# Graph network kernel: where the marks of the lanes are made, and ten instead of eight of GpSimd's 25 partial sums

## The chip, the cores and the metric

The kernel runs on one core of a Trainium2 chip. The time is that of the whole program in microseconds, the median of several executions. In profiles the engines are called PE (TensorE, matrix products), DVE (VectorE), ACT (ScalarE), POOL (GpSimd) and SP (SyncE, which only issues transfers here). PEld is the loading of TensorE's weights.

## What is computed

A graph of 3125 nodes with 128 features and 100,000 edges, sorted by their destination, goes through a mean layer, three attention layers, an aggregation layer with four statistics (PNA) and two more mean layers. The change touches the first mean layer and the bookkeeping that the later passes need from it:

```python
h = relu(layernorm(x))
agg = segment_sum(h[src], dst)               # mean over a node's incoming edges
deg = segment_sum(ones, dst)                 # how many edges a node has
mean = agg / max(deg, 1)
x = x + relu(where(deg > 0, mean, h) @ W.T + b)
# then three times:
h = attention(h, src, dst)                   # softmax over a node's incoming edges
```

## The kernel before, in words

**First mean pass.** The edges have first been turned into a matrix of counts, A (source by destination), which lies in DRAM. The pass reads A in seven blocks, 0 to 6: six of 512 destination nodes (four tiles of 128 nodes, 6400 KB) and one of 128. Two buffers in SBUF take turns; a buffer is loaded again when TensorE, VectorE and GpSimd have all read it. Inside a block, the 25 source tiles lie side by side. Per block:

- TensorE multiplies features by counts over the 25 source tiles (`neighbour_sums`, line 1043), then sums the column sums over the partitions with a matrix of ones into `psL` (line 1139: every partition then holds the in-degrees of the block's nodes as a row) and, transposed, into `psS` (line 1142: degrees as columns), then makes the previous block's outputs tile by tile (`node_outputs`, lines 1056 and 1057). Two PSUM banks take turns for the tiles, so the third tile of a block waits until VectorE has used up the first.
- VectorE sums 17 of the 25 source tiles per destination (`degrees`, line 1540), GpSimd the other 8 (lines 647 and 650, seven adds), and VectorE puts the two together (line 1545). Then VectorE works on the block before: `segments`, then `outputs` (lines 1579 to 1581, three instructions a tile), then `moments` (lines 1332 and 1335) for the next layer norm.
- ScalarE copies TensorE's sums out of PSUM (`sums_out`, line 753).

**The marks.** Every one of the 128 partitions ("lanes") later works on 784 consecutive edges. `pick` says for each lane and node whether the node's last edge lies in the next lane, that is, whether the node's edges cross the lane's end. `segments` makes it from a running sum of the degree row: a scan (line 1554), a carry (1556), a difference (1557), three comparisons (1561 to 1563). The scan and the difference read the row in `psL`. Between them and after them stand the small operations on the degrees as columns (`deg`, `has`, `nohas`, `hrec`). After the pass TensorE turns `pick` into one number a node, the crossing flag (line 1152, 25 products, `psH`), and VectorE makes `cbias` of it (line 1629). `pick` is first used by the pass after that at the end of the first attention pass.

**Attention pass.** Each of the three attention passes has 56 groups of 14 steps of all lanes, four groups a round, in four slots of SBUF; two groups are a pair. GpSimd fetches the source rows of a group by indirect transfers (line 695), 12 of the 14 steps in even slots, 11 in odd ones. TensorE fetches the rest of a pair from SBUF by one-hot products (`fetch`, line 1187), whose one-hot matrices ScalarE (`own_hots`, lines 871 and 876) and VectorE (line 1694) make. VectorE reduces the fetched rows (line 1718), makes the logits (lines 1743 to 1760), ScalarE takes their exponentials (line 900), and VectorE runs the recurrence over the steps (lines 1768 to 1778). The order on each engine is the order of the code. The indices of a slot reach GpSimd through ScalarE (`window`, lines 851 to 854): those of slots 0 and 1 ahead of the pass, those of slot 2 in ScalarE's group 0, ahead of its exponential, and those of slot 3 in its group 1, so behind the exponential of group 0.

Of the kernel before, what the change touches and what calls it, by code (L numbers as in the profile page):

```python
# [29 lines left out]
POOL_S = 8  # L30
# [63 lines left out]
def build(nc, x, src, dst, W0, b0, Ws, Wd, att_s, att_d, gat_b, M_w, M_b, U_w, U_b, gamma, beta,  # L94
# [37 lines left out]
    with ExitStack() as ctx:  # L132
# [97 lines left out]
        psF = [psT[0], psT[1], psY[0], psY[1], psL, psZ, psS]  # L230
        cw_p = psH[:, 0:15 * H].rearrange("p (h k) -> p h k", h=H)
# [163 lines left out]
        dense_ps, mb_rdy, red_rdy, deg_ps = sem("dense_ps"), sem("mb_rdy"), sem("red_rdy"), sem("deg_ps")  # L395
        deg_used, node_out_ps, node_out = sem("deg_used"), sem("node_out_ps"), sem("node_out")
# [318 lines left out]
        def _(act):  # L715
# [83 lines left out]
            for b in range(NBK):  # L799
                sums_out(0, b)  # L800
            act.wait_ge(deg_rdy, 1)
# [218 lines left out]
        def _(pe):  # L1020
# [111 lines left out]
            for b in range(NBK + 1):  # L1132
                if b < NBK:
                    neighbour_sums(0, b, u)
                    n = blocks[b][1] * W
                    pe.wait_ge(red_rdy, b + 1)
                    if b:
                        pe.wait_ge(deg_used, b)
                    nc.tensor.matmul(psL[:, 0:n], ones[:], reds[b % 2][:, 0:n], start=True, stop=True)
                    for t in tiles(b):  # L1140
                        k = t - TPB * b
                        ins = nc.tensor.matmul(psS[:, 32 + t:33 + t], reds[b % 2][:, k * P:(k + 1) * P], ones[:, 0:1],
                                               start=True, stop=True)
                    ins.then_inc(deg_ps, 1)
                if b:
                    node_outputs(0, b - 1)
# [3 lines left out]
            pe.wait_ge(pick_rdy, NBK)  # L1150
            for t in range(NT):
                ins = nc.tensor.matmul(psH[:, t:t + 1], pick_t(t), ones[:, 0:1], start=True, stop=True)
            ins.then_inc(cross_ps, 1)
            pe.wait_ge(node_out, NT)

            for p in passes:
# [55 lines left out]
                if p.by_pe:  # L1212
                    pe.wait_ge(split_rdy, p.splits0 + 5)
                    for q in range(p.groups // 2):
                        fetch(q)

# [93 lines left out]
        def _(dve):  # L1310
# [236 lines left out]
            def segments(b):  # L1547

                a, n = blocks[b][0] * W, blocks[b][1] * W
                at = slice(tiles(b)[0], tiles(b)[-1] + 1)  # L1550
                dve.wait_ge(deg_ps, b + 1)
                if b:
                    dve.wait_ge(node_out, tiles(b - 1)[-1] + 1)
                link(v.tensor_tensor_scan(upto[:, 0:n], ones[:, 0:1].broadcast_to([P, n]), psL[:, 0:n], carry[:, 0:1],
                                          ALU.mult, ALU.add))
                link(v.tensor_copy(carry[:], upto[:, n - 1:n]))
                link(v.tensor_tensor(since[:, 0:n], upto[:, 0:n], psL[:, 0:n], ALU.subtract))
                link(v.tensor_copy(deg[:, at], psS[:, 32 + at.start:32 + at.stop]))
                v.tensor_scalar(tmp[:, 0, at], deg[:, at], 1.0, None, ALU.max).then_inc(deg_used, 1)
                pk = pick[:, a:a + n]  # L1560
# [3 lines left out]
                dve.wait_ge(deg_used, b + 1)  # L1564
                v.tensor_scalar(has[:, at], deg[:, at], 0.0, None, ALU.is_gt)
                link(v.reciprocal(tmp[:, 0, at], tmp[:, 0, at]))
                link(v.tensor_scalar(nohas[:, at], has[:, at], -1.0, 1.0, ALU.mult, ALU.add))
                link(v.tensor_tensor(hrec[:, at], tmp[:, 0, at], has[:, at], ALU.mult))
# [33 lines left out]
            dve.wait_ge(pick_rdy, NBK)  # L1602
            v.tensor_copy(tmp[:, 0, :], deg[:]).then_inc(deg_rdy, 1)

# [23 lines left out]
            dve.wait_ge(cross_ps, 1)  # L1628
            link(v.tensor_scalar(cbias[:], psH[:, 0:NT], -1.0, BIG, ALU.add, ALU.mult))

            for p in passes:
# [168 lines left out]
                if p.by_pe:  # L1800
                    own_hots(0, 0)
                    own_hots(0, 1)
                    own_hots(1, 0)
                if p.pairs:
# [44 lines left out]
                en = ends(p)  # L1849
                if p.kind == GAT:  # L1850
# [124 lines left out]
```

## Time and profile before

| | |
|---|---|
| median of three runs | 5052.01 us (5048.47 to 5052.94) |
| the profiled execution | 5046.86 us, of which the profile's span is 5045.0 us |
| busy: PE, DVE, ACT, POOL | 3624.6, 3952.3, 2562.6, 2820.5 us |
| granted clock of TensorE | 0.858 of full speed, mean |
| first mean pass | from about 616 to 814 us |
| first attention pass, from its table to its last state | from about 826 to 1702 us |

A row of a timeline has the start and the duration in microseconds, the engine, the line of the kernel, the operation with the tile that it writes and those that it reads, and the number of instructions merged in the row. In brackets stands how long the engine had been idle, and who ended that.

### The profile page before, as it was taken

How to read it: one execution, taken by the hardware profiler on the slowest of the kernel's cores; microseconds unless marked ns; L12 is line 12 of the kernel's file. 1: busy time of each engine (PE TensorE's matmuls, PEld its weight loads, DVE VectorE, ACT ScalarE, POOL GpSimd, SP SyncE). 2: the span in 40 equal slices, each digit the busy share in tenths (PEclk: the TensorE clock that was granted, in tenths of full speed). 3: DMA queues.
4: the chain of work that ended last, by engine and by line, in shares of the span. 5: the costliest groups of instructions: out<-in, count | busy, mean ns of one | idle time of the engine just before them, and what ended most of it. 6: DMA issues, size and time to landing. Idle time of an engine off the chain costs nothing.

```text
span 5045.0 us, 64486 instructions
## 1 busy us (share of the span) xinstructions
PE 3624.6 (72%) x17056; PEld 1885.1 (37%) x17056; DVE 3952.3 (78%) x10821; ACT 2562.6 (51%) x6428; POOL 2820.5 (56%) x2909
## 2 busy tenths in 40 slices
PE   6999795888888478888856888886433433337799
PEld 3444344444444234444433444443211111114444
DVE  8999886898888679888876988887798888884211
ACT  5878603555455245544424554453487777773100
POOL 0000034777777677777767777776477777772000
PEclk9999897999899689889977999997677666768899
DMA  4444561344444334444433444433277777772566
GB/s 167 157 154 153 205 223 51 115 137 129 133 134 125 91 110 138 125 134 132 130 100 90 136 129 133 133 125 122 68 288 279 275 281 287 282 277 67 208 236 219
DMA packets 323829, 817.06 MB, mean 162 GB/s; under 512 B 80800, under 2 KB 239552, under 8 KB 308677
## 3 DMA queue, kind: packets, MB, share of 16 engines
q1 hardware_dynamic: 201244, 594.04, 31.2%
q0 software_dynamic: 92336, 200.10, 14.9%
q10 hardware_dynamic: 29944, 19.32, 1.5%
q8 instruction: 136, 2.23, 0.2%
q14 instruction: 169, 1.38, 0.1%
HBM read 350.23 MB, written 462.98 MB: 161 GB/s over the span
## 4 chain that ended last, share of the span: by engine, by line
POOL 31%; DVE 19%; issue 16%; PE 14%; ACT 5%; DMA 5%; SPq 3%; POOLq 0%; ACTq 0%; DVEq 0%
POOL big L695 29%; PE psT L1043 7%; DVE big L1778 4%; DMA big<-table,src_win 3%; DVE big L1791 2%; DVE big L1694 2%; DVE big L1768 2%; SPq L511 2%; PE psY L1267 1%; SPq L512 1%; DVE big L1718 1%; PE psY L1187 1%; PE psS L1209 1%; ACT hT L884 1%; POOL big L709 1%
## 5 line engine op out<-in xcount | busy, mean ns | idle before, releaser
L695 POOL DMA_INDIRECT big<-table,src_win x2660 | 2560.6, 963 | 883.1 <-issue 773.2
L1778 DVE SCALAR_TENSOR_TENSOR big<-big,keep_win 128x132 f32<-128x132 f32 x2184 | 781.7, 358 | 77.8
L1209 PE MATMUL psS<-big,hT 128*128 128x384 bf16 x1400 | 352.2, 429 | 548.9 <-DVE hT L1703 548.9
L871 ACT ACTIVATE hT<-src_bc,node_c 128x640 bf16<-128x640 f16 x840 | 621.2, 814 | 144.5 <-PE psL L1187 80.0
L900 ACT ACTIVATE psH<-d_b 128x60 f32<-128x60 f32 x168 | 37.6, 224 | 1167.9 <-DVE d_b L1760 1167.9
L1187 PE MATMUL psT<-big 128*128 128x408 bf16 x1800 | 488.6, 337 | 53.3 <-DVE big L1694 53.3
L1187 PE MATMUL psY<-big 128*128 128x408 bf16 x1800 | 488.4, 336 | 0.0
L876 ACT ACTIVATE hT<-hT 128x3200 bf16<-128x3200 bf16 x168 | 482.2, 2870 | 5.4
L1187 PE MATMUL psT<-big,hT 128*128 128x408 bf16 x1200 | 378.9, 379 | 143.6 <-DVE big L1718 72.6
L1187 PE MATMUL psY<-big,hT 128*128 128x408 bf16 x1200 | 378.9, 380 | 98.2 <-DVE big L1718 69.1
L1209 PEld LDWEIGHTS psS<-big,hT 128*128 128x128 bf16 x1400 | 169.1, 124 | 731.8 <-issue 693.6
L1694 DVE TENSOR_SCALAR big<-src_bc,node_c 128x640 bf16<-128x640 f16 x1260 | 408.7, 395 | 20.3 <-PE psL L1187 20.3
L647 POOL TENSOR_TENSOR dst_i<-big 128x512 f32<-128x512 f32 (+1 forms) x7 | 8.1, 1150 | 689.1 <-DMA big<-A_d 609.4
L1768 DVE TENSOR_TENSOR big<-big,psH 128x1848 f32<-128x1848 f32 x168 | 349.4, 2080 | 28.5 <-ACT psH L900 27.3
L1187 PE MATMUL psL<-big 128*128 128x408 bf16 x900 | 302.6, 336 | 0.0
L1187 PE MATMUL psZ<-big 128*128 128x408 bf16 x900 | 301.5, 335 | 0.0
L1187 PE MATMUL psS<-big 128*128 128x408 bf16 x900 | 301.5, 335 | 0.0
L1043 PE MATMUL psT<-big 128*128 128x512 f32 (+1 forms) x700 | 277.4, 557 | 5.4 <-issue 4.8
L1187 PE MATMUL psS<-big,hT 128*128 128x408 bf16 x600 | 227.3, 379 | 57.5 <-DVE big L1718 41.5
L1187 PE MATMUL psZ<-big,hT 128*128 128x408 bf16 x600 | 227.7, 380 | 52.6 <-DVE big L1718 44.1
L1187 PE MATMUL psL<-big,hT 128*128 128x408 bf16 x600 | 228.9, 382 | 48.3 <-DVE big L1718 40.5
L789 ACT ACTIVATE big<-psT 128x400 bf16<-128x400 f32 x496 | 233.0, 503 | 55.1 <-PE psT L1103 48.4
(368 smaller groups left out, 7377.7 us busy)
## 6 DMA issues: line engine op xcount, KB each, us to landing
rows<-big SPq DMA_DIRECT2D x112, 1792.0 KB
rows<-big SPq DMA_DIRECT2D x168, 952.0 KB
big<-A_d SPq DMA_DIRECT2D x17, 6400.0 KB, 19.3
A_d<-big SPq DMA_DIRECT2D x396, 200.0 KB, 1.9
big<-table,src_win POOLq DMA_INDIRECT x2660
big<-A_d SPq DMA_DIRECT2D x7, 1600.0 KB, 6.9
src_bc<-pe_src_d ACTq DMA_DIRECT2D x84, 128.0 KB, 2.8
table<-big SPq DMA_DIRECT2D x15, 350.0 KB, 2.9
```

The costliest lines, as they stand in the source:

```text
L511: to = sp.value_load(blk[0:1, bass.ds(rnd * STATES + z, 1)], min_val=0, max_val=DUMP + STEPS - 1)
L695: pool.indirect_dma_start(out=rows[:, k, 0:p.table_w], out_offset=None, in_=table, in_offset=bass.IndirectOffsetOnAxis(ap=src_win[:, s, k: ...
L789: nc.scalar.activation(hot_q[:, t % HOTS, j, :], psD[(dist0[t] + n) % 4][:, 0:QW], ACT.Relu).then_inc(hot_s, 1)
L871: ins = nc.scalar.activation(hot_of[t], src_bc[:, q % 2, :], ACT.Square, bias=node_c[:, t:t + 1], scale=-1.0)
L876: nc.scalar.activation(at, at, ACT.Relu, bias=1.0, scale=-1.0).then_inc(is_src_rdy, 1)
L1043: ins = nc.tensor.matmul(psT[at % 2][:, 0:n * W].rearrange("f (b w) -> f b w", w=W), rows[:, s, :], abuf[(at + 1) % 2][:, 0:n, W * s:W * s ...
L1187: ins = nc.tensor.matmul(psF[j % BANKS][:, 0:3 * w].rearrange("p (c w) -> p c w", c=3), hot_of[t][:, i * P:(i + 1) * P], table_s[:, t, :, ...
L1209: ins = nc.tensor.matmul(psS[:, 0:3 * D].rearrange("p (c w) -> p c w", c=3), is_src[:, t, 0:P], table_s[:, t, :, 0:D], start=(n == 0), sto ...
L1694: ins = v.tensor_scalar(hot_of[t], src_bc[:, q % 2, :], node_c[:, t:t + 1], None, ALU.is_equal)
L1768: v.tensor_tensor(for_heads, for_heads, over_heads(by_edge(cw_p[:, :, 1:15]), HC), ALU.mult).then_inc(chained, 1)
L1778: v.scalar_tensor_tensor(state[:, k, 0:GATW], prev[k][:, 0:GATW], kw[:, 0, k:k + 1], rows[:, k, 0:GATW], ALU.mult, ALU.add).then_inc(chain ...
L1791: v.scalar_tensor_tensor(state[:, k, 0:2 * D], prev[k][:, 0:2 * D], kw[:, 0, k:k + 1], psR[k][:, 0:2 * D], ALU.mult, ALU.add).then_inc(upd ...
```

## The change

`segments` keeps only the operations on the degrees as columns, four small ones per block; two more are done once for all 25 tiles after the pass. The marks are a function of their own, `lane_marks`, which reads the degree row from a copy in `pick` itself. ScalarE makes the copy in the mean pass, after `sums_out`. VectorE calls `lane_marks` for all seven blocks in the first attention pass, after its three `own_hots` and ahead of group 0. TensorE's 25 products over `pick` and VectorE's `cbias` go to the end of that pass; the products write another bank (`cross_p`). GpSimd sums ten source tiles, VectorE 15.

```diff
-POOL_S = 8
+POOL_S = 10
...
+        cross_p = psS[:, 480:480 + NT]
...
             for b in range(NBK):
+                a, n = blocks[b][0] * W, blocks[b][1] * W
                 sums_out(0, b)
+                act.wait_ge(deg_ps, b + 1)
+                nc.scalar.copy(pick[:, a:a + n], psL[:, 0:n]).then_inc(deg_row_rdy, 1)
...
                     if b:
                         pe.wait_ge(deg_used, b)
+                        pe.wait_ge(deg_row_rdy, b)
...
-            pe.wait_ge(pick_rdy, NBK)
-            for t in range(NT):
-                ins = nc.tensor.matmul(psH[:, t:t + 1], pick_t(t), ones[:, 0:1], start=True, stop=True)
-            ins.then_inc(cross_ps, 1)
             pe.wait_ge(node_out, NT)
...
                     for q in range(p.groups // 2):
                         fetch(q)
+                if p.number == 0:
+                    pe.wait_ge(pick_rdy, NBK)
+                    pe.wait_ge(fetched_rdy, p.fetched0 + p.groups // 2 * PAIR_ROWS)
+                    for t in range(NT):
+                        ins = nc.tensor.matmul(cross_p[:, t:t + 1], pick_t(t), ones[:, 0:1], start=True, stop=True)
+                    ins.then_inc(cross_ps, 1)
...
             def segments(b):
...
                 dve.wait_ge(deg_ps, b + 1)
+                link(v.tensor_copy(deg[:, at], psS[:, 32 + at.start:32 + at.stop]))
+                v.tensor_scalar(nohas[:, at], deg[:, at], 0.0, None, ALU.is_equal)
+                link(v.tensor_scalar(hrec[:, at], deg[:, at], 1.0, None, ALU.max))
+                v.reciprocal(hrec[:, at], hrec[:, at]).then_inc(deg_used, 1)
+                dve.wait_ge(deg_used, b + 1)
+
+            def lane_marks(b):
+                a, n = blocks[b][0] * W, blocks[b][1] * W
+                pk = pick[:, a:a + n]
+                dve.wait_ge(deg_row_rdy, b + 1)
+                link(v.tensor_tensor_scan(upto[:, 0:n], ones[:, 0:1].broadcast_to([P, n]), pk, carry[:, 0:1],
                                           ALU.mult, ALU.add))
                 link(v.tensor_copy(carry[:], upto[:, n - 1:n]))
+                link(v.tensor_tensor(since[:, 0:n], upto[:, 0:n], pk, ALU.subtract))
                 link(v.tensor_scalar(pk, since[:, 0:n], lane_last[:, 0:1], None, ALU.is_lt))
...
-            dve.wait_ge(pick_rdy, NBK)
             v.tensor_copy(tmp[:, 0, :], deg[:]).then_inc(deg_rdy, 1)
+            link(v.tensor_scalar(has[:], nohas[:], -1.0, 1.0, ALU.mult, ALU.add))
+            link(v.tensor_tensor(hrec[:], hrec[:], has[:], ALU.mult))
...
                     own_hots(1, 0)
+                if p.number == 0:
+                    for b in range(NBK):
+                        lane_marks(b)
...
                 en = ends(p)
+                if p.number == 0:
+                    dve.wait_ge(cross_ps, 1)
+                    link(v.tensor_scalar(cbias[:], cross_p, -1.0, BIG, ALU.add, ALU.mult))
```

VectorE in one block of the mean pass, before. The names in brackets are the semaphores that a row waits for.

```order
L1540 TENSOR_REDUCE lane_x<-big 128x512 [waits a_in0,deg_ps]
L1545 TENSOR_TENSOR lane_x<-lane_x,dst_i 128x512 [waits part_sum,dve_chain]
L1554 SCALAR_TENSOR_TENSOR lane_s<-ones,carry,psL 128x512 [waits node_out,deg_ps]
L1556 COPY carry<-lane_s 128x1 [waits dve_chain]
L1557 TENSOR_TENSOR Z<-lane_s,psL 128x512 [waits dve_chain]
L1558 COPY deg<-psS 128x4 [waits dve_chain]
L1559 TENSOR_SCALAR tmp<-deg 128x4 [waits dve_chain]
L1561 TENSOR_SCALAR pick<-Z,lane_last 128x512
L1562 SCALAR_TENSOR_TENSOR pick<-lane_s,lane_last,pick 128x512 [waits dve_chain]
L1563 SCALAR_TENSOR_TENSOR pick<-lane_s,lane_last,pick 128x512 [waits dve_chain]
```

The same block on VectorE in the changed kernel, up to the first output tile.

```order
L1549 TENSOR_REDUCE lane_x<-big 128x512 [waits a_in0,deg_ps]
L1554 TENSOR_TENSOR lane_x<-lane_x,dst_i 128x512 [waits part_sum,dve_chain]
L1560 COPY deg<-psS 128x4 [waits deg_ps]
L1561 TENSOR_SCALAR nohas<-deg 128x4 [waits dve_chain]
L1562 TENSOR_SCALAR hrec<-deg 128x4
L1563 RECIPROCAL hrec<-hrec 128x4 [waits dve_chain]
L1589 SCALAR_TENSOR_TENSOR lane_s<-psY,hrec,rowb 128x128 [waits node_out_ps,deg_used]
```

Six operations over the width of the block have left it. They stand now on VectorE in the attention pass, ahead of group 0; the changed kernel has there, at the end of the last block's marks:

```order
L1571 SCALAR_TENSOR_TENSOR lane_s<-ones,carry,pick 128x128 [waits deg_row_rdy,pick_rdy]
L1573 COPY carry<-lane_s 128x1 [waits dve_chain]
L1574 TENSOR_TENSOR Z<-lane_s,pick 128x128 [waits dve_chain]
L1575 TENSOR_SCALAR pick<-Z,lane_last 128x128 [waits dve_chain]
L1576 SCALAR_TENSOR_TENSOR pick<-lane_s,lane_last,pick 128x128 [waits dve_chain]
L1577 SCALAR_TENSOR_TENSOR pick<-lane_s,lane_last,pick 128x128 [waits dve_chain]
L1726 TENSOR_REDUCE big<-psT 128x136 [waits fetched,pick_rdy]
```

The last row is the first of group 0: it reduces what TensorE fetched, and stood directly behind `own_hots` before.

TensorE between the passes, before:

```order
L1149 MATMUL psS<-deg,ones 128x25
L1152 MATMUL psH<-ones,pick 128x1 [waits pick_rdy]
L1152 MATMUL psH<-ones,pick 128x1 x24
L1026 MATMUL psT<-ident,big 128x128 [waits u_rdy,node_out]
L1026 MATMUL psT<-ident,big 128x128 x3
```

and at the end of the first attention pass in the changed kernel, behind the last of the one-hot products:

```order
L1189 MATMUL psS<-big 128x408
L1223 MATMUL psS<-ones,pick 128x1 [waits fetched_rdy,pick_rdy]
L1223 MATMUL psS<-ones,pick 128x1 x24
L1234 MATMUL psL<-ident,lane_x 128x128 [waits laneL_rdy]
L1234 MATMUL psL<-ident,lane_x 128x128 x2
```

The 25 products over `pick` are gone from between the two passes, and stand ahead of the wait for the lanes' last states.

## Rows read from the trace of the kernel before

**Rows 1.** The chain that ended last, on the page: share of the span by engine and line.
```profile
POOL big L695 29%; PE psT L1043 7%; DVE big L1778 4%; DMA big<-table,src_win 3%; DVE big L1791 2%; DVE big L1694 2%; DVE big L1768 2%; SPq L511 2%; PE psY L1267 1%; SPq L512 1%; DVE big L1718 1%; PE psY L1187 1%; PE psS L1209 1%; ACT hT L884 1%; POOL big L709 1%
```

**Rows 2.** DVE's timeline, one block of the pass: start us, us, engine, line, operation [idle].
```profile
705.68 14.88 DVE L1540 TENSOR_REDUCE lane_x<-big 128x512 f32<-128x8704 f32 x1
...
721.20 1.27 DVE L1554 TENSOR_TENSOR_SCAN lane_s<-ones,carry,psL 128x512 f32<-128x512 f32 x1
...
724.49 1.64 DVE L1562 SCALAR_TENSOR_TENSOR pick<-lane_s,lane_last,pick 128x512 f32<-128x512 f32 x1
...
730.52 0.35 DVE L1579 SCALAR_TENSOR_TENSOR lane_s<-psY,hrec,rowb 128x128 f32<-128x128 f32 x1
```

**Rows 3.** PE's timeline over the pass.
```profile
645.83 21.70 PE L1043 MATMUL psT<-big 128*128 128x512 f32 x50
...
669.04 0.47 PE L1056 MATMUL psY<-wT,big 128*128 128x128 f32 x2
...
673.64 23.25 PE L1043 MATMUL psT<-big 128*128 128x512 f32 x50
...
703.00 22.22 PE L1043 MATMUL psT<-big 128*128 128x512 f32 x50
725.07 1.02 PE L1139 MATMUL psL<-lane_x,ones 128*128 128x512 f32 x2
...
726.73 0.47 PE L1056 MATMUL psY<-wT,big 128*128 128x128 f32 x2
...
733.80 22.18 PE L1043 MATMUL psT<-big 128*128 128x512 f32 x50
...
788.26 0.47 PE L1056 MATMUL psY<-wT,big 128*128 128x128 f32 x2
...
791.70 5.75 PE L1043 MATMUL psT<-big 128*128 128x128 f32 x50
```

**Rows 4.** GpSimd's timeline, the adds of one block.
```profile
722.77 8.84 POOL L650 TENSOR_TENSOR dst_i<-dst_i,big 128x512 f32<-128x512 f32 x6
```

**Rows 5.** The page on DMA issues: count, KB each, us to landing.
```profile
big<-A_d SPq DMA_DIRECT2D x17, 6400.0 KB, 19.3
```

**Rows 6.** DVE's timeline at the end of the pass.
```profile
794.55 3.82 DVE L1540 TENSOR_REDUCE sm<-big 128x128 f32<-128x2176 f32 x1
...
798.61 1.27 DVE L1554 TENSOR_TENSOR_SCAN lane_s<-ones,carry,psL 128x512 f32<-128x512 f32 x1
...
800.83 0.16 DVE L1558 COPY deg<-psS 128x4 f32<-128x4 f32 x1
...
801.62 0.75 DVE L1562 SCALAR_TENSOR_TENSOR pick<-lane_s,lane_last,pick 128x512 f32<-128x512 f32 x1
...
803.07 0.16 DVE L1565 TENSOR_SCALAR has<-deg 128x4 f32<-128x4 f32 x1
...
813.71 0.15 DVE L1603 COPY tmp<-deg 128x25 f32<-128x25 f32 x1
```

**Rows 7.** PE's timeline between the passes.
```profile
814.79 10.80 PE L1152 MATMUL psH<-ones,pick 128*128 128x1 f32 x50
```

**Rows 8.** ACT's timeline between the passes.
```profile
826.59 0.60 ACT L733 ACTIVATE hT<-psT 128x512 f32<-128x512 f32 x1 [0.49 <-PE psT L1026]
```

**Rows 9.** DVE's timeline where the attention pass begins.
```profile
894.12 2.53 DVE L1694 TENSOR_SCALAR big<-src_bc,node_c 128x640 bf16<-128x640 f16 x8 [6.55 <-PE psL L1187]
904.39 1.07 DVE L1718 TENSOR_REDUCE big<-psT 128x136 f32<-128x408 f32 x2 [7.75 <-PE psL L1187]
```

**Rows 10.** ACT's timeline, same place.
```profile
908.74 0.22 ACT L900 ACTIVATE psH<-d_b 128x60 f32<-128x60 f32 x1 [6.38 <-DVE d_b L1760]
...
916.25 0.19 ACT L851 COPY src_win<-src_i 128x14 int32<-128x14 int32 x1
```

**Rows 11.** GpSimd's timeline: the fourth slot's first gather, and the pass's end.
```profile
916.70 0.94 POOL L695 DMA_INDIRECT big<-table,src_win  x1 [0.93 <-ACT src_win L851]
...
1701.85 0.94 POOL L709 DMA_INDIRECT big<-rows,end_i  x1 [16.80 <-DMA rows<-big]
```

More of the change, by code:

```diff
@@ L395, in build @@
         dense_ps, mb_rdy, red_rdy, deg_ps = sem("dense_ps"), sem("mb_rdy"), sem("red_rdy"), sem("deg_ps")
+        deg_row_rdy = sem("deg_row_rdy")
         deg_used, node_out_ps, node_out = sem("deg_used"), sem("node_out_ps"), sem("node_out")
@@ L1547, in segments @@
             def segments(b):
-                a, n = blocks[b][0] * W, blocks[b][1] * W
                 at = slice(tiles(b)[0], tiles(b)[-1] + 1)
                 dve.wait_ge(deg_ps, b + 1)
-                if b:
-                    dve.wait_ge(node_out, tiles(b - 1)[-1] + 1)
-                link(v.tensor_tensor_scan(upto[:, 0:n], ones[:, 0:1].broadcast_to([P, n]), psL[:, 0:n], carry[:, 0:1],
+                link(v.tensor_copy(deg[:, at], psS[:, 32 + at.start:32 + at.stop]))
[8 more added lines that the diff above has]
+                link(v.tensor_tensor_scan(upto[:, 0:n], ones[:, 0:1].broadcast_to([P, n]), pk, carry[:, 0:1],
                                           ALU.mult, ALU.add))
                 link(v.tensor_copy(carry[:], upto[:, n - 1:n]))
[L1557 to L1560, printed above, removed]
+                link(v.tensor_tensor(since[:, 0:n], upto[:, 0:n], pk, ALU.subtract))
                 link(v.tensor_scalar(pk, since[:, 0:n], lane_last[:, 0:1], None, ALU.is_lt))
@@ L1563, in segments @@
                 v.scalar_tensor_tensor(pk, upto[:, 0:n], lane_last[:, 1:2], pk, ALU.is_le, ALU.mult).then_inc(pick_rdy, 1)
[L1564 to L1568, printed above, removed]
+                dve.wait_ge(pick_rdy, b + 1)
             def outputs(m, b):
@@ L1627, in _ @@
             link(v.tensor_scalar(nohas[:], has[:], -1.0, None, ALU.mult))
-            dve.wait_ge(cross_ps, 1)
-            link(v.tensor_scalar(cbias[:], psH[:, 0:NT], -1.0, BIG, ALU.add, ALU.mult))
             for p in passes:
```

## The prediction

> **What bounds the kernel now.** I read the page's chain first: its largest part is GpSimd's issue of gathers in the passes over the edges, line 695, with TensorE's line 1043 (the mean passes) second [rows 1]. The change touches one mean pass and one attention pass, so I then read the timelines of the engines in those two places.
>
> In the first mean pass VectorE sets the pace. TensorE starts blocks 3 and 4 at 703.00 and 733.80, 30.8 us apart, though its own products take 22.1 of them; block 4 starts late because the output tiles before it wait for VectorE [rows 3]. VectorE meanwhile goes without a gap from the reduction (14.9 us) over the sum to `segments`, from 721.2 to 730.5, 9.3 us, and only then to the outputs [rows 2].
>
> In the attention pass GpSimd sets the pace. From the first gather of slot 3 in round 0, at 916.70, to the last one of the pass lie 609 gathers (28 pairs of 23, less 35 in slots 0 to 2), and the next row is at 1701.85 after 16.80 us of idle time, so the last ends at 1685.05: 1.26 us each with their gaps, and I found no gap above the usual 0.3 us between them. GpSimd's first of these waited for `src_win`, ScalarE's copy at 916.25 [rows 10, 11]. That copy stands behind ScalarE's exponential at 908.74, which waited 6.38 us for VectorE's `d_b` of group 0. So group 0 on VectorE holds GpSimd's fourth slot, and there is no slack: GpSimd had come to it 0.6 us before.
>
> **The change in the mean pass.** VectorE's block loses the marks and two of 17 source tiles: 14.9 x 15/17 = 13.1 us remain of the reduction, 0.7 for the sum, under 1 us for four small operations, some 5 for the outputs and 1.5 for the moments, together 21 to 23 us. That is less than TensorE's own path, which sets the pace next: products 22.1 (21.7 at the least), degree sums 1.7 (725.07 to 726.73), output tiles. The tiles took 4.6 us with GpSimd adding at that time (669.04 to 673.64) and 3.4 without (788.26 to 791.70) [rows 3]. So a block takes 27.2 to 28.4 us; I take 27.6, nearer to the middle, since GpSimd's sum now ends later and lies beside part of the tiles.
>
> GpSimd makes nine adds a block in place of seven. Six take 8.84 us [rows 4], so nine are 13.3 us, begun when VectorE has finished a block's counts and needed a block later: hidden by 27.6 - 13.3 = 14 us. A load needs 19.3 us [rows 5] and starts when TensorE is done with the buffer, a block and the tiles ahead of its need: hidden too. ScalarE's copy of the row is of the shape of its copy in `sums_out`, once a block, in an engine that idles there; even at VectorE's 1.27 us for a scan of that width it lies beside TensorE's next products.
>
> Blocks 0 to 2 are set by loads and TensorE, and stay. Block 3 starts at 702.5 (703.0 less 0.5 by which VectorE was late), block 6 three blocks later at 785.3 in place of 791.70: 6.4 us earlier. The bounds are 788.2 (three times 28.4 from 703.0) and 783.4 (three times 27.2 from 701.8), so 3.5 to 8.3 us.
>
> The end of the pass: from the start of block 6 on TensorE to VectorE's copy at 813.71 are 22.0 us [rows 3, 6]. The reduction of 3.82 becomes 3.37. `segments` of block 5 (from 798.61, over 4.5 us) no longer stands ahead of block 5's tiles, but TensorE, which waits for it, needs 2.4 us more to bring the first, so 1.8 us are won; `segments` of block 6, 2.9 us before, becomes some 0.8. Sum: 0.4 + 1.8 + 2.1 = 4.3 us; bounds 3 and 5.5.
>
> TensorE's 25 products over `pick` (10.8 us) [rows 7] go from between the passes. They lie beside ScalarE's normalising, and ScalarE waits only 0.49 us for TensorE after it [rows 8]: I take 0.4 us, bounds 0 and 0.8. At their new place TensorE has fetched everything and waits for two more groups of VectorE, which is over 20 us: free. Should that cover be gone, they would cost 10.8.
>
> Together the attention pass begins 6.4 + 4.3 + 0.4 = 11.1 us earlier (6.5 to 14.6).
>
> **The change in the attention pass.** The marks of a block of 512 take, undisturbed, from 798.61 to 803.07, less the two small degree operations between (0.16 at 800.83 and one like it, partly overlapped): 4.25 us [rows 6]. Six are 25.5. The narrow block lies between a quarter of that, 1.1, and the whole; I take 2.1, since half of its operations' time does not shrink with the width. Sum 27.6 us. They start when `own_hots` ends, at 894.12 + 2.53 = 896.65 on the old clock, and VectorE then waited 7.75 us for TensorE before group 0 [rows 9]. So 27.6 - 7.7 = 19.9 us are not covered. Bounds: 17.5 and 23.
>
> What is queued behind them: group 0 on VectorE, so ScalarE's exponential, so its copy of slot 3's indices, so GpSimd's gathers from slot 3 on. GpSimd is the pace of this pass and has no idle time later in which to make up. Slot 2 is filled early and does not help, because its 12 gathers are already done by then. TensorE's second fetch is held as well, since its banks are free only after VectorE's first reductions, but VectorE needs it a whole pair later. The whole delay reaches the end of the pass.
>
> **Sum.** 19.9 - 11.1 = +8.8 us: the profiled execution's 5046.9 us becomes 5055.7. It lies 5 us under the median of the runs shown, 5052.0, which becomes 5060.8.
>
> **A rule weighed.** An operation of the marks with two SBUF inputs, line 1562, took 1.64 us while GpSimd was adding and 0.75 when it was not [rows 2, 6]. The Trainium skill, "SBUF — State Buffer", section "Who interferes with whom", says that a VectorE instruction with two SBUF inputs contends with a GpSimd instruction that reads SBUF, and one with at most one such input (outside the two-port modes) does not. The trace agrees: line 1579, which reads one input from PSUM, stays at 0.35. By that rule the marks might meet GpSimd again in the attention pass, where it reads indices for its gathers; there only slot 2's 12 gathers, 15 us at 1.26, fall beside the marks before GpSimd stands still, so I price this as a rival and not in the sum.
>
> **The rivals.**
> 1. The delay is made good (faster). VectorE runs ahead of GpSimd's gathers later in the pass, so 20 us of VectorE might be swallowed there, if GpSimd went on issuing meanwhile. Then only the 11.1 us remain: 5052.0 - 11.1 = 5040.9. For it: the page lists GpSimd first in the chain and VectorE behind. Against it: slot 3's indices came behind group 0's exponential already [rows 10, 11]. Chance 0.09.
> 2. The mean pass gains nothing (slower). TensorE's third and fourth tile of a block wait for VectorE's last operation on the first and second, which has two SBUF inputs and can be held by an add of GpSimd, up to 1.3 us each; now that GpSimd adds for 13 us from the middle of TensorE's products on, every block would meet it. The tiles then take 3.4 + 2.6 = 6.0 us, a block 29.8, and block 6 starts at 703.0 + 89.4 = 792.4, 0.7 later than now. The gain falls to 4.3 + 0.4 - 0.7 = 4.0, and the time is 5052.0 + 15.9 = 5067.9. It decides from a block of 28.0 us on: then the sum passes +10.1 us. Chance 0.12.
> 3. The marks are held by the gathers (slower). If both comparisons of the six wide blocks took 1.64 in place of 0.75, that would be 12 x 0.89 = 10.7 us; slot 2's gathers lie beside about half of the marks, so 5.3 us more: 5066.1, and 5071.5 at the most. Against it: no row shows a gather that holds VectorE. Chance 0.05.
> 4. VectorE still paces the mean pass, for its block stays above 28 us. It needs 5 us more than I count; no row shows them. In with the second.
>
> **How the numbers follow.** The forecast's mechanism has 0.72, the rivals 0.09, 0.12 and 0.05, and 0.02 is left for no change from some other cause. A measurement of this kernel can tell about 0.2%, 10.1 us, from no change. The likeliest case gives +8.8 with its own range +5 to +13 (5057 to 5065), since corners of the bounds seldom meet; about two thirds of it lie below 10.1. So: within 0.2% 0.48 from it plus 0.03 from the rest and 0.01 of the rivals, 0.52; slower by over 0.2% 0.24 + 0.11 + 0.04, 0.39; faster 0.09. The range for 8 in 10 reaches from 5053 to 5068: it takes in the second rival and the third's likelier half, and leaves the first outside.
>
> **What would show it.** The step in the mean pass is right if TensorE's line of the products starts blocks 27 to 28.4 us apart and VectorE's copy of the degrees after the pass comes near 802.6, with VectorE idle in every block. The marks are right if VectorE's seven blocks last 27 to 28 us, the first reduction of group 0 comes at about 912.7 in place of 904.39, GpSimd shows one wait of some 20 us ahead of slot 3, and that slot starts at about 925.5. The pass then ends, at GpSimd's first gather of last rows, near 1710.5 instead of 1701.85, and all later passes are moved by the same 8.8 us. It is wrong if GpSimd's wait at slot 3 is much shorter than VectorE's delay, or if the pass's end moves less than its slot 3 does. TensorE's 25 products must end before the lanes' last states are ready; if the transposes behind them wait for them, the free step was not free.

## The result and the profile after

| | before | changed |
|---|---|---|
| median of 22 runs each | 5050.82 us (5047.09 to 5055.07) | 5057.31 us (5049.78 to 5067.26) |
| ratio of the changed kernel to before | | 1.0013, 95% interval 1.0007 to 1.0019 |
| span of the profiled execution | 5045.0 us | 5054.9 us |

The change costs 6.5 us, 0.13%, with an interval of 3.5 to 9.6 us: the time rises, but by less than the 0.2% that was taken as the bound for "no change". The forecast was +8.8 us, 5060.8 against the 5052.01 of the first three runs.

The whole trace up to the mean pass ran some 2.3 us earlier than before (block 1 of TensorE's products starts at 643.53 in place of 645.83 [rows 3]). What is changed ahead of it is the sum of block 0, and TensorE doesn't wait for that; kernels with either form of the mean pass start block 1 anywhere from 642.0 to 645.8. So starts are compared from block 1 on.

TensorE's timeline over the mean pass, changed kernel; columns as in rows 3, in brackets the idle time before and who ended it.

```profile
643.53 21.70 PE L1048 MATMUL psT<-big 128*128 128x512 f32 x50
...
700.05 21.62 PE L1048 MATMUL psT<-big 128*128 128x512 f32 x50
721.51 1.02 PE L1145 MATMUL psL<-lane_x,ones 128*128 128x512 f32 x2
...
726.92 21.62 PE L1048 MATMUL psT<-big 128*128 128x512 f32 x50
...
754.96 22.13 PE L1048 MATMUL psT<-big 128*128 128x512 f32 x50
...
782.04 5.75 PE L1048 MATMUL psT<-big 128*128 128x128 f32 x50
```

Blocks 3 to 6 are now 26.9, 28.0 and 27.1 us apart. Before, blocks 3 and 4, and 4 and 5, stood 30.8 apart [rows 3], and 5 and 6 stood 27.1 apart already, so two distances have shrunk. VectorE has room in each block:

```profile
702.77 13.19 DVE L1549 TENSOR_REDUCE lane_x<-big 128x512 f32<-128x7680 f32 x1
715.99 0.69 DVE L1554 TENSOR_TENSOR lane_x<-lane_x,dst_i 128x512 f32<-128x512 f32 x1
716.60 0.16 DVE L1560 COPY deg<-psS 128x4 f32<-128x4 f32 x1
716.79 0.17 DVE L1561 TENSOR_SCALAR nohas<-deg 128x4 f32<-128x4 f32 x1
716.87 1.25 DVE L1562 TENSOR_SCALAR hrec<-deg 128x4 f32<-128x4 f32 x1
718.15 0.18 DVE L1563 RECIPROCAL hrec<-hrec 128x4 f32<-128x4 f32 x1
723.98 0.35 DVE L1589 SCALAR_TENSOR_TENSOR lane_s<-psY,hrec,rowb 128x128 f32<-128x128 f32 x1 [5.65 <-PE psY L1062]
...
797.61 0.14 DVE L1612 COPY tmp<-deg 128x25 f32<-128x25 f32 x1
```

The reduction is 13.2 us in place of 14.9 [rows 2], and ahead of the outputs VectorE waits 5.65 us for TensorE. The last row answers to the copy at 813.71 [rows 6].

The marks on VectorE in the attention pass: the end of `own_hots`, the first block, the last one, and the first row of group 0. It answers to rows 9, where the reduction stood at 904.39.

```profile
877.51 2.69 DVE L1702 TENSOR_SCALAR big<-src_bc,node_c 128x640 bf16<-128x640 f16 x8 [6.66 <-PE psL L1189]
880.12 1.27 DVE L1571 TENSOR_TENSOR_SCAN lane_s<-ones,carry,pick 128x512 f32<-128x512 f32 x1
...
882.86 0.75 DVE L1576 SCALAR_TENSOR_TENSOR pick<-lane_s,lane_last,pick 128x512 f32<-128x512 f32 x1
...
884.44 1.29 DVE L1571 TENSOR_TENSOR_SCAN lane_s<-ones,carry,pick 128x512 f32<-128x512 f32 x1
...
906.09 0.48 DVE L1571 TENSOR_TENSOR_SCAN lane_s<-ones,carry,pick 128x128 f32<-128x128 f32 x1
...
908.21 1.07 DVE L1726 TENSOR_REDUCE big<-psT 128x136 f32<-128x408 f32 x2
```

And GpSimd in the changed kernel: the first transfer after the mean pass, a gather of slot 2 beside the marks, the first of slot 3, and the pass's end. They answer to rows 11; between the first and the third lie 107.98 us.

```profile
812.54 1.02 POOL L665 DMA_INDIRECT start_ad<-big,start_i  x1 [35.83 <-ACT big L823]
...
888.28 1.27 POOL L697 DMA_INDIRECT big<-table,src_win  x1 [0.30 <-issue]
...
920.52 0.94 POOL L697 DMA_INDIRECT big<-table,src_win  x1 [19.56 <-ACT src_win L856]
...
1706.73 0.94 POOL L711 DMA_INDIRECT big<-rows,end_i  x1 [17.20 <-DMA rows<-big]
```

One wait of 19.56 us stands there, where before it was 0.93 [rows 11]. Before, the first transfer after the mean pass started at this row:

```profile
829.25 1.02 POOL L663 DMA_INDIRECT start_ad<-big,start_i  x1 [42.03 <-ACT big L818]
```

So the mean pass and what follows it up to there took 169.0 us from block 1 (812.54 - 643.53) in place of 183.4: 14.4 won. From there to slot 3 are 108.0 us in place of 87.5 (916.70 - 829.25): 20.5 lost. Net 6.1 up to slot 3, against 6.5 in the timed runs.

The two spans differ by 9.9 us, and that is not the price of the change: 2.3 us are saved ahead of block 1, 7.2 lost from there to the end of the pass, and 5.0 lost behind it, where the two kernels have the same code. Over the ten traces taken on the faster chips that last stretch took from 3342 to 3356 us, so 5 us in it are chance.

### The profile page after: what moved, and what is told of

The parts are those of the page before. It is cut to its first block, busy times and chain, and to the rows that moved or that the text cites. A ratio compares the mean times of both kernels' runs of the same rounds, so it can differ in the third digit from the quotient of the medians.

```text
span 5054.9 us, 64496 instructions
## 1 busy us (share of the span) xinstructions
PE 3614.5 (72%) x17056; PEld 1880.9 (37%) x17056; DVE 3935.3 (78%) x10809; ACT 2564.2 (51%) x6435; POOL 2835.7 (56%) x2923
## 3 DMA queue, kind: packets, MB, share of 16 engines
q0 software_dynamic: 92336, 200.10, 14.9%
## 4 chain that ended last, share of the span: by engine, by line
POOL 29%; PE 17%; DVE 17%; issue 14%; ACT 6%; DMA 5%; POOLq 0%; ACTq 0%; DVEq 0%
POOL big L697 28%; PE psT L1048 8%; DVE big L1786 3%; DMA big<-table,src_win 3%; DVE big L1799 2%; DVE big L1702 2%; PE psT L1189 2%; DVE big L1776 1%; PE psY L1276 1%; PE psY L1189 1%; ACT hT L889 1%; DVE big L1726 1%; PE psS L1211 1%; ACT big L728 1%; DVE hT L1711 1%
## 5 line engine op out<-in xcount | busy, mean ns | idle before, releaser
L1702 DVE TENSOR_SCALAR big<-src_bc,node_c 128x640 bf16<-128x640 f16 x1260 | 409.2, 396 | 21.9 <-PE psL L1189 21.5
```

Of the source, the lines that this page charges most:

```text
L1702: ins = v.tensor_scalar(hot_of[t], src_bc[:, q % 2, :], node_c[:, t:t + 1], None, ALU.is_equal)
```

## The experiments

Theory A is the forecast's: marks ahead of group 0 hold GpSimd's fourth slot for their whole uncovered time, and TensorE paces the mean pass. B is in each case the rival named in the expectation. "From block 1" means from the start of TensorE's second block to GpSimd's first transfer after the mean pass (183.4 us before, 169.0 changed); "the pass" from that transfer to GpSimd's first gather of last rows (872.6 before, 894.2 changed). The pass of kernels without marks in it came out at 872.6, 874.0, 875.6 and 875.7, so 3 us in it are chance.

### The price of the marks

Without any marks: `pick` is filled with zeros, so the crossing flags, and what rests on them in the output, are left out.

```diff
                 if p.number == 0:
-                    for b in range(NBK):
-                        lane_marks(b)
+                    dve.wait_ge(deg_row_rdy, NBK)
+                    v.memset(pick[:], 0.0).then_inc(pick_rdy, NBK)
```

> Left out: the marks; pick is set to zero by one memset in their place, so cbias has one value for all nodes. The change otherwise whole. Theory A (what the marks leave uncovered goes whole to the end of the pass): the memset fits in the 7.7 us in which VectorE waits there anyway, GpSimd's wait ahead of slot 3 falls from 19.6 us to about 1, and the kernel is 20.5 us faster than the changed one, about 5037 us, ratio to the kernel before 0.9972. Theory B (the delay is made good later in the pass, and the loss comes from elsewhere): at most 8 us faster than the changed kernel, 5049 or more.

Measured: 5040.16 us against 5052.26 of before on the same chip, ratio 0.9974 (0.9965 to 0.9983), so -12.1 us. Taken with the changed kernel's +6.5, the marks cost 18.6 us, with some 5 us to each side; the pass itself is 18.6 us shorter in the trace (875.6 in place of 894.2). GpSimd at its fourth slot in this kernel:

```profile
815.54 1.02 POOL L665 DMA_INDIRECT start_ad<-big,start_i  x1 [37.85 <-ACT big L823]
...
903.47 0.94 POOL L697 DMA_INDIRECT big<-table,src_win  x1 [0.94 <-ACT src_win L856]
```

87.93 us lie between the two rows, as before the change; the 19.56 us of wait are 0.94. A holds: the whole loss comes from the marks in that place, and what is left is the gain ahead of it.

### Is it the indices, or VectorE's delay itself?

ScalarE copies slot 3's indices in its group 0, ahead of the exponential that waits for VectorE.

```diff
-                        window(rnd, s + 2)
+                        if not (p.number == 0 and type(rnd) is int and rnd == 0 and s == 1):
+                            window(rnd, s + 2)
+                        if p.number == 0 and type(rnd) is int and rnd == 0 and s == 0:
+                            window(rnd, 3)
```

> The changed kernel, but in the first attention pass ScalarE copies slot 3's indices together with slot 2's, ahead of group 0's exponential. Theory A (it is group 0 on VectorE that holds everything, by whichever semaphore comes next): slot 3 starts some 19 us earlier, directly behind slot 2, and GpSimd then waits about 17 us ahead of slot 0 of round 1, whose indices need VectorE's update of group 0 and stand behind group 1's exponential; 2 to 3 us faster than the changed kernel, 5054 to 5055 us. Theory B (the place of this one copy is the hold): 19 us faster, about 5038 us, with no wait of over 2 us behind slot 3.

Measured: 5058.88 us, ratio 1.001 (1.0001 to 1.0019). Slot 3 is now filled without a wait, and the wait comes one slot later, 15.27 us long:

```profile
917.17 0.95 POOL L697 DMA_INDIRECT big<-table,src_win  x1 [0.30 <-issue]
933.38 0.96 POOL L697 DMA_INDIRECT big<-table,src_win  x1 [15.27 <-ACT src_win L856]
```

The pass lasts 893.5 us, 0.7 less, and the time shows nothing of the 2 to 3 us that A gave to it (its interval reaches 4.5 us to each side); B, with 19 us, falls. The slots are all full then, and a slot comes free only when VectorE has used a group: the copy at `src_win` was where the delay showed, not what made it.

### Eight tiles on GpSimd in the changed kernel

```diff
-POOL_S = 10
+POOL_S = 8
```

> The changed kernel with 8 instead of 10 of the source tiles on GpSimd. Theory A (TensorE sets the pace of the mean pass once the marks are gone): blocks still start 27 to 28 us apart, only the last reduction is 0.45 us longer; no change beyond 1 us, 5057 to 5058 us. Theory B (the shift to GpSimd carries part of the gain): VectorE's 1.7 us more a block show in four blocks, 6 to 7 us slower, 5064 us.

Measured: 5059.42 us, ratio 1.0017 (1.0008 to 1.0026), where the changed kernel has 1.0013. From block 1 it takes 168.95 us (645.12 to 814.07), as with ten, and blocks 3 to 6 are 27.2, 27.6 and 26.6 apart. That is A: TensorE paces the blocks once the marks have left them. The tail is 0.8 us longer (16.4 in place of 15.6), and TensorE's granted clock is 1.00 in all three blocks, so a worth of a microsecond can't be read from one trace; the 6 to 7 us of B are not there.

### Ten tiles alone, and the 25 products alone

Each is the kernel before with one part of the change: `POOL_S = 10`; or the products and `cbias` at the end of the attention pass.

> The kernel before with nothing changed but that GpSimd sums ten source tiles and VectorE 15. The marks stay in the mean pass. A (the kernel is now as fast as its parts say): VectorE still paces a block of the mean pass, and its reduction is 1.75 us shorter, so a block is about 1 to 1.75 us shorter where VectorE paces it; the attention pass begins 4 to 5 us earlier and nothing is given back: before - 4 us. B (the shorter block is given back, or GpSimd's two more adds hold VectorE's small operations): within 1.5 us of before.

> The kernel before with nothing changed but that the 25 products over pick and cbias stand at the end of the first attention pass, not between the passes. A (the forecast's term): the products lay beside ScalarE's normalising and gain 0 to 0.8 us; before - 0.5 us. B (they were on the path between the passes, and account for what the gain ahead of the attention pass was above the forecast, 3.3 us): the first scatter comes 3 us earlier behind VectorE's copy of the degrees, and the time is before - 3 us or more.

Measured: ten tiles alone 5049.92 us against 5053.67, ratio 0.9992 (0.9983 to 1.0001); the products alone 5050.92, ratio 0.9996 (0.9987 to 1.0006). Both intervals hold no change and both hold A, and only the trace says more. With ten tiles alone, VectorE in a block (as rows 2):

```profile
701.63 13.19 DVE L1540 TENSOR_REDUCE lane_x<-big 128x512 f32<-128x7680 f32 x1
...
715.47 1.27 DVE L1554 TENSOR_TENSOR_SCAN lane_s<-ones,carry,psL 128x512 f32<-128x512 f32 x1
...
718.76 1.64 DVE L1562 SCALAR_TENSOR_TENSOR pick<-lane_s,lane_last,pick 128x512 f32<-128x512 f32 x1
...
724.80 0.35 DVE L1579 SCALAR_TENSOR_TENSOR lane_s<-psY,hrec,rowb 128x128 f32<-128x128 f32 x1
```

`segments` still takes 9.3 us, and the reduction is 1.7 us shorter. But blocks 3 to 6 start 29.9, 30.8 and 29.0 us apart, together 89.7. Before it was 88.7, and 89.8 in the trace of the products alone, whose mean pass is that of before: at this size the distances vary with TensorE's granted clock (0.97, 0.89 and 0.91 with ten tiles; 0.89, 0.89 and 0.94 with the products alone; 0.94, 0.94 and 0.98 before). In the middle one of the three distances VectorE is no longer the only bound. TensorE needs 24.0 us to its degree sums (728.45 to 752.41), and VectorE waits for it:

```profile
754.88 0.35 DVE L1579 SCALAR_TENSOR_TENSOR lane_s<-psY,hrec,rowb 128x128 f32<-128x128 f32 x1 [0.68 <-PE psY L1057]
```

The tile's last instruction, line 1581, then takes 1.18 us with GpSimd adding beside it (at 755.65), where it took 0.47 before (at 762.11). From block 1 to the copy of the degrees the kernel takes 167.6 us, against 167.9 before and 169.1 with the products alone, so ten tiles alone won 0.3 to 1.5 us, not the 4 to 5 of A.

With the products moved alone, GpSimd's first transfer comes 14.93 us after VectorE's copy of the degrees (811.13 to 826.06), in place of 15.54 (813.71 to 829.25); in the changed kernel it is 14.93 too (797.61 to 812.54). So they were worth 0.6 us, and B, which wanted 3, falls by the trace. At their new place they run in a gap:

```profile
1669.25 10.80 PE L1217 MATMUL psS<-ones,pick 128*128 128x1 f32 x50 [5.21 <-DVE big L1719]
1696.16 0.90 PE L1228 MATMUL psL<-ident,lane_x 128*128 128x128 f32 x3 [16.11 <-DVE lane_x L1821]
```

TensorE still waits 16.11 us behind them.

### Other places for the marks

Late: one block of marks after each of the rounds 5 to 11 of the same pass, run on two chips.

```diff
-                if p.number == 0:
-                    for b in range(NBK):
-                        lane_marks(b)
...
                     for s in range(SLOTS):
                         group(rnd, s)
+                    if p.number == 0 and 5 <= rnd < 5 + NBK:
+                        lane_marks(rnd - 5)
```

> The changed kernel, but VectorE makes the marks of one block after each of the rounds 5 to 11 of the first attention pass, not all ahead of group 0. Theory A (GpSimd sets the pace of the pass, and VectorE idles ahead of its gathers from round 4 on): the marks' 27.7 us vanish in VectorE's waits, GpSimd's wait ahead of slot 3 is about 1 us; its gathers beside the marks are a little longer (1.2 instead of 0.95 us, 3 us in sum): 5040 us, ratio to the kernel before 0.998. Theory B (VectorE's work counts wherever it stands in the pass): slower than the changed kernel by the 7.7 us of cover that are lost, 5065 us.

> The changed kernel with one block of marks after each of the rounds 5 to 11 of the attention pass, once more, beside the one with the marks in the gaps. A (the gathers are slower beside the marks, and only that is lost): before - 7 us, as it was, 5 us above the kernel without marks. B (the earlier gain was chance of the single programs' loading): within 2 us of before.

Gaps: the first block behind the outputs of the mean pass's first block, two blocks between the passes behind the last small operation on the degrees, four after the rounds 5 to 8.

```diff
                     segments(b - 1)
...
+                    if b == 1:
+                        lane_marks(0)
...
             link(v.tensor_scalar(nohas[:], has[:], -1.0, None, ALU.mult))
+            lane_marks(1)
+            lane_marks(2)
...
+                    if p.number == 0 and 5 <= rnd < 2 + NBK:
+                        lane_marks(rnd - 2)
```

> The changed kernel with the marks spread: the first block's in the mean pass behind a block's outputs, two blocks' between the passes, and the other four after rounds 5 to 8 of the attention pass, one after each. A (what costs is only that the marks stand ahead of group 0): the 19.6 us of the changed kernel's marks are nearly all won back, and less of them lies beside the gathers than with all seven in the pass: before - 9 us, 2 us below marks late. B (each place costs its own share, since VectorE between the passes is on the path to the first gather): before - 5 us or above, so no better than marks late.

Measured: late 5044.79 us against 5052.26 (ratio 0.9985, 0.9976 to 0.9994), and again 5047.43 against 5053.67 (the same ratio and interval); gaps 5044.43 against 5053.67, ratio 0.998 (0.9971 to 0.999). Both beat both kernels. Spread out, the marks no longer stop GpSimd; what they still cost is in GpSimd's gathers that run beside them. A's 5040 us for the late marks was too low: it counted 3 us for the slower gathers, where the pass shows 5.3. Late (second run), one block of marks on VectorE, and GpSimd at that time:

```profile
1224.28 1.27 DVE L1571 TENSOR_TENSOR_SCAN lane_s<-ones,carry,pick 128x512 f32<-128x512 f32 x1
...
1227.81 0.75 DVE L1577 SCALAR_TENSOR_TENSOR pick<-lane_s,lane_last,pick 128x512 f32<-128x512 f32 x1
```

```profile
1224.89 1.42 POOL L697 DMA_INDIRECT big<-table,src_win  x1 [0.31 <-issue]
1226.61 1.19 POOL L697 DMA_INDIRECT big<-table,src_win  x1 [0.30 <-issue]
1228.11 1.27 POOL L697 DMA_INDIRECT big<-table,src_win  x1 [0.30 <-issue]
1229.68 0.94 POOL L697 DMA_INDIRECT big<-table,src_win  x1 [0.30 <-issue]
```

Three gathers take 1.42, 1.19 and 1.27 us in place of 0.94, 1.06 us a block of marks; in the first run the first of the three took 1.78 beside two of the blocks. The pass lasts 880.9 us late (881.1 in the first run) and 877.6 with gaps, against 875.6 without marks: 5.3 and 2.0 more, with seven and with four blocks beside gathers, where 3 us are chance. The two blocks between the passes cost nothing: GpSimd's first transfer comes 14.93 us after the copy of the degrees (797.01 to 811.94), as in the changed kernel. A holds for the gaps (-9.2 us, forecast -9), though the times alone don't part them from late: they are 3.0 us apart with intervals of 4.5 us to each side. The bound without marks is -12.1.

The second run of the late marks shows how far the mean pass varies. Its code there is that of the changed kernel, but from block 1 it takes 174.0 us in place of 169.0, with blocks 3 to 6 at 30.0, 28.1 and 28.3 us apart. In the first of these TensorE's granted clock is 0.90 in place of 1.00, its products take 23.2 us in place of 21.5, and the tiles 5.2 in place of 3.7, the last instruction of the first tile (line 1591, at 725.91) being held for 1.17 us beside GpSimd's adds. In the first run of the same kernel it was 169.1.

### Four kernels on another chip

Ten tiles alone, the products alone, the gaps and a mix (the first five blocks behind the outputs of the mean pass, the last two between the passes, none in the attention pass) were run first, before the runs above, on a chip where the kernel before took 6667.12 us.

> The kernel before, with 10 instead of 8 source tiles on GpSimd and nothing else. Theory A (VectorE still sets the pace of the mean pass, so its reduction counts, but GpSimd's longer sum holds its port longer): 1.7 us less in four blocks and 0.45 in the last, less up to 2 us for operations of the marks that meet an add: 3 to 7 us faster than the kernel before, 5046 to 5049 us. Theory B (TensorE already sets the pace): no change, 5052 us.

> The kernel before, with only TensorE's 25 products over pick and VectorE's cbias moved to the end of the first attention pass. Theory A (the products lie beside ScalarE's normalising): the first scatter comes 0 to 1 us earlier and nothing else changes; no difference that can be measured, 5051.5 us. Theory B (TensorE's transposes and projections between the passes wait for them and hold ScalarE): up to 8 us faster, 5044 us.

> The changed kernel with the marks in VectorE's idle time: block 0 in the mean pass after segments of block 0 (VectorE idles 10 us there), blocks 1 and 2 between the passes (11.9 us idle), blocks 3 to 6 after rounds 5 to 8 of the attention pass. Theory A: no marks on the path, and fewer beside gathers than with all seven late: 2 to 3 us faster than all marks late, ratio to the kernel before 0.998, about 5042 us. Theory B (what marks cost beside gathers is no matter): the same as with all marks late, 5045.

> The changed kernel with the marks of blocks 0 to 4 in the mean pass, from ScalarE's copy, ahead of the output tiles, where VectorE idles 5 to 8 us a block, and blocks 5 and 6 between the passes. Theory A: with GpSimd adding beside them the marks of a block take about 6.5 us, 1 to 2 us more than the idle time in one or two blocks; the attention pass holds none: 18 us faster than the changed kernel, ratio to the kernel before 0.9975, 5040 us. Theory B (VectorE again sets the pace of the mean pass): blocks 2 to 5 back at 30 us, first scatter at 822 or later, no faster than 5045 us.

Measured, as ratios to before there: ten tiles alone 1.0004 (0.9953 to 1.0055), products alone 1.0036 (1.0 to 1.0071), gaps 1.003 (0.9995 to 1.0064), mix 1.0054 (1.0019 to 1.0089). The attention passes have another bound there. The longest waits of ten tiles alone (engine, line, who ended it, total us, times, longest):

```profile
ACT psH L900 <- DVE d_b L1760: 2054.3, 89, 27.6
DVE big L1718 <- remote: 1359.2, 74, 19.8
POOL big L695 <- DVE big L1778: 1089.0, 65, 17.4
```

GpSimd waits for VectorE up to 17.4 us, again and again, and VectorE for something that the trace doesn't name. A sum that rests on GpSimd's pace can't be tested there, so these times decide nothing on it, and the first three have a second run, above. The mean pass looked as elsewhere, and the mix can be read there. VectorE with marks behind the small operations of a block, GpSimd adding beside it:

```profile
748.35 2.15 DVE L1571 TENSOR_TENSOR_SCAN lane_s<-ones,carry,pick 128x512 f32<-128x512 f32 x1
...
750.73 1.39 DVE L1574 TENSOR_TENSOR Z<-lane_s,pick 128x512 f32<-128x512 f32 x1
752.15 1.38 DVE L1575 TENSOR_SCALAR pick<-Z,lane_last 128x512 f32<-128x512 f32 x1
753.56 1.64 DVE L1576 SCALAR_TENSOR_TENSOR pick<-lane_s,lane_last,pick 128x512 f32<-128x512 f32 x1
...
756.91 0.35 DVE L1589 SCALAR_TENSOR_TENSOR lane_s<-psY,hrec,rowb 128x128 f32<-128x128 f32 x1
```

The marks of a block take 8.6 us (748.35 to 756.91), twice the 4.3 of the attention pass and more than A's 6.5, and TensorE's blocks 4 and 5 are 30.4 us apart (730.11 to 760.56), blocks 3 to 6 together 89.4. So the gain of the blocks is gone, as B has it. That of the tail is kept (16.0 us), and from block 1 to the first transfer are 177.8 us, between the 169.0 of the changed kernel and the 183.4 of before. The scan took 1.27 when it read the row in PSUM [rows 2] and takes 2.15 from `pick`. The Trainium skill, "SBUF — State Buffer", section "Who interferes with whom", has VectorE contend with GpSimd's reads when both its inputs are in SBUF; by it the copy of the row into SBUF turns two more operations of the marks, the scan and the difference (line 1574), into such ones, and the rows agree.

## Why the prediction was right

The sum was +19.9 - 11.1 = +8.8; the trace up to slot 3 has +20.5 - 14.4 = +6.1, and the timed runs +6.5, with an interval (3.5 to 9.6) that holds the forecast. The mechanism and both signs were right. The gain was sized 3.3 us too small for this trace. In the seven traces of the changed mean pass taken on the faster chips (the gaps, with one block of marks in it, among them) it lies between 9.4 and 15.2 us (168.2 to 174.0 in place of 183.4), so part of the 3.3 is the luck of one trace; the tail is not.

- **Blocks of the mean pass.** Forecast 27.6 us a block and 6.4 won by block 6. Measured 27.3 (81.99 in three) and 7.4: 0.7 up to block 3, 6.7 after it. What was less than forecast were the products: 21.5, 21.5 and 22.0 us to the degree sums, where 22.1 was taken. The tiles took 3.7, 4.9 and 3.4 us, 4.0 on average, where 3.8 was taken. The four small operations on VectorE took 1.7 us beside GpSimd's adds, not under 1, which costs nothing, since VectorE waits behind them.
- **The tail.** This is the term that was mis-sized: forecast 4.3 (bounds 3 and 5.5), measured 6.4, 22.0 us down to 15.57; in the other traces with ten tiles and this tail 15.6 to 16.0, so 6.0 at the least. By the rows of the two timelines of VectorE it splits so: the reduction 0.4 (forecast 0.4); from the sum to the first output 5.1 us down to 2.0, so 3.2 (forecast 1.8); the four tiles 0.6 (forecast none); `segments` of block 6 2.2 (forecast 2.1). In the view by stretches (stretch, its length, busy time of PE, PEld, DVE, ACT and POOL with counts, granted clock, DMA share, GB/s) the tail is, before and changed:

```profile
791.70:813.70 22.00, 12.04 (x76) 10.97 (x74) 20.31 (x66) 1.55 (x2) 0.00 (x0) 0.68 0.00 0
```

```profile
782.04:797.60 15.56, 9.43 (x76) 8.53 (x74) 13.42 (x50) 1.81 (x3) 0.00 (x0) 0.98 0.00 1
```

  TensorE's granted clock is 0.68 there before and 0.98 now, where 0.50 and 1.00 are its two levels of 1.2 and 2.4 GHz. Ahead of its degree sums it stood idle for 3.89 us before and for 1.49 now. Its degree sums and its first tile, before and changed:

```profile
801.34 0.77 PE L1139 MATMUL psL<-sm,ones 128*128 128x128 f32 x2 [3.89 <-DVE tmp L1559]
...
802.18 0.78 PE L1056 MATMUL psY<-wT,big 128*128 128x128 f32 x2
802.75 0.63 PE L1057 MATMUL psY<-wT,hT 128*128 128x128 f32 x2
```

```profile
789.27 0.46 PE L1145 MATMUL psL<-sm,ones 128*128 128x128 f32 x2 [1.49 <-DVE sm L1554]
...
789.71 0.47 PE L1061 MATMUL psY<-wT,big 128*128 128x128 f32 x2
790.02 0.39 PE L1062 MATMUL psY<-wT,hT 128*128 128x128 f32 x2
```

  From the start of the sums to the end of the first tile are 2.04 us before (801.34 to 803.38) and 1.14 changed (789.27 to 790.41). So of the 1.4 us by which the first output came earlier than forecast, 0.9 are the clock. The rest is that VectorE was still in `segments` when the tile was ready before, so that the forecast's 2.4 us for TensorE held some 0.3 us that were VectorE's own, and that the small operations took some 0.2 us less than was priced. The forecast did have the wait of the sums for VectorE's column operations; what it took over without a question was the time of TensorE's products from the trace of before. Of the 0.6 us of the four tiles about 0.4 go with the clock as well: where it was lower behind the first tile (0.80 over the tail, in the second run of the late marks), they took 4.3 us in place of 3.9. Why the clock was higher at the sums was not tested; it was in the seven traces in which TensorE had stood idle for 1.5 to 1.9 us there, and with ten tiles alone after 3.5 us, and it was low in the two traces with 3.9 us.
- **The 25 products.** Forecast 0.4, measured 0.6, free at their new place, by two traces.
- **The marks.** Forecast 27.6 us on VectorE, measured 28.1 (880.12 to 908.21), less the 7.7 that were covered, 20.4: the loss up to slot 3 is 20.5, forecast 19.9. They are 4.33 us a block in place of 4.25, and the narrow one is 2.1 as taken. Without them the time falls by 18.6 us, with some 5 us to each side.
- **Given back later?** The first rival wanted the delay made good. From slot 3 to the end of the pass are 785.15 us before, 786.21 changed and 787.62 without marks, so nothing came back that stands out of the 3 us of chance; and the changed indices show that the delay only moves to the next slot.
- **The second rival**, blocks of over 28.0 us: in this trace one of the three was 28.0, the others shorter. Its mechanism is there: an add of GpSimd holds VectorE's last operation on a tile (line 1591, 0.66 and once 0.93 us for 0.29), and the block with tiles of 4.9 us is the one of 28.0. In the second run of the late marks all three were over 28.0, with a lower clock beside it. So this rival came nearer than the one trace shows.
- **The third rival**, marks held by gathers: the sign of the contention was the other way. Lines 1576 and 1577 stayed at 0.75 us, and the gathers went to 1.27. Where they only fill slot 2 this is hidden; where the marks stand among gathers that set the pace it costs some 1 us a block.
- **The ten tiles** were priced inside VectorE's block, not on their own; with eight no difference of the changed kernel can be measured.

## What to carry to other kernels

When work is moved off one engine's bound stage into another stage, look for what is queued behind it there at the start, not at the mean load: VectorE had room for 28 us in the attention pass, but not ahead of its first group, where the engine with the longest queue stands ready and can't catch up. The same work after the pipeline is full cost some 5 us in place of 19, and split over real gaps 2 to 3. And when a wait goes from the bound stage, the granted clock of the engine that waited may change, so durations read from its products in the old trace are open both ways: the tail here got the higher clock, and a block in the second run of the late marks the lower one.

## What the runs showed of the hardware

- A VectorE operation on 4 elements took 1.25 us while GpSimd was adding (line 1562 of the changed kernel, at 716.87) and 0.16 when it was not (in the tail); the copy ahead of it, which reads PSUM, stayed at 0.16. The operation ahead of it, of the same kind, started before GpSimd's first add (at 716.83) and took 0.17; the reciprocal at 718.15, beside an add, took 0.18. So it was not the size that was paid for: an add of GpSimd over 128 by 512 takes 1.3 us. In the next to last block the add covers 128 by 128 and takes 0.45 us, and line 1562 beside it 0.44 (at 772.05). The Trainium skill, "SBUF — State Buffer", section "Who interferes with whom", says that a VectorE `tensor_scalar` in a two-port mode and GpSimd lock each other out for a whole instruction; the 1.25 us beside an add of 1.26, and 0.44 beside 0.45, agree.
- Operations of the marks lengthen gathers of GpSimd from 0.94 to 1.19, 1.27 and 1.42 us, at three places to 1.78 or 1.79, and are not lengthened themselves beyond 0.02 us. Which of the operations does it was not taken apart.
- All runs on one chip lay 32% above those on the others, with a mean granted clock of 0.77 in place of 0.86 and with the time going into waits inside the attention passes; GpSimd's gathers still took 0.96 us each.
